# The batch loops of an eight-stage kernel written out, and every wait on a constant

## The reference: what is computed

```python
x = x + tanh(g_xattn[0]) * L0_xattn(ctx, layernorm(x), ...)   # s0: state-space scan over 256 steps
x = x + tanh(g_ffn[0])   * L0_ffn(layernorm(x), ...)          # s1: 8 experts, top 2, and a shared one
x = x + tanh(g_xattn[1]) * L1_xattn(layernorm(x), fside, ctx) # s2: int8-quantised gated product
x = x + tanh(g_ffn[1])   * L1_ffn(layernorm(x), ...)          # s3: ternary SwiGLU
x = x + tanh(g_xattn[2]) * L2_xattn(layernorm(x), ctx, ...)   # s4, sa: 16-head attention
x = x + tanh(g_ffn[2])   * L2_ffn(layernorm(x), ...)          # s5: ternary weights, int8 activations
x = x + tanh(g_xattn[3]) * L3_xattn(layernorm(x), ctx, ...)   # s6: one-head attention
x = x + tanh(g_ffn[3])   * L3_ffn(layernorm(x), ...)          # s7: ternary SwiGLU with a norm
```

## Time and profile before

| | |
|---|---|
| median of 3 runs | 1250.54 us |
| the profiled execution | 1251.78 us |
| its span, first to last instruction | 1249.6 us |
| PE busy | 840.5 us (67%), 4052 matmuls |
| DVE busy | 831.5 us (67%), 1944 instructions |
| ACT busy | 493.4 us (39%), 1242 instructions |
| POOL busy | 371.2 us (30%), 412 instructions |
| mean granted TensorE clock | 0.812 |
| instruction packets | 56 of 8 KB on queue q14, 17 of 16 KB on q8 |

### The profile page before, as it was taken

One profiled execution on the slowest core, in us unless ns is written; L12 is line 12 of the kernel. 1 busy time (PEld: TensorE's weight loads), 2 busy tenths in 40 slices (PEclk: granted clock), 3 DMA queues, 4 the chain that ended last, 5 costly groups with the idle time before them and its releaser, 6 DMA issues.

```text
span 1249.6 us, 15616 instructions
## 1 busy us (share of the span) xinstructions
PE 840.5 (67%) x4052; PEld 618.9 (50%) x4052; DVE 831.5 (67%) x1944; ACT 493.4 (39%) x1242; POOL 371.2 (30%) x412
## 2 busy tenths in 40 slices
PE   2114863587338853785469797879789697888756
PEld 1003641465126621673256585657567485667535
DVE  4896789569875889467630596439863596439763
ACT  2421422224212422243137554545365454555332
POOL 4744362317322553212020122131123212131123
PEclk9555985689558965798589898989999897999857
DMA  3150000010001000023210000010000100000000
GB/s 130 67 233 13 0 1 1 1 47 0 0 0 47 0 0 0 18 84 139 78 53 22 13 1 6 1 35 1 4 1 0 35 0 5 0 21 1 1 0 9
DMA packets 12185, 33.43 MB, mean 27 GB/s; under 512 B 2120, under 2 KB 5584, under 8 KB 10320
## 3 DMA queue, kind: packets, MB, share of 16 engines
q1 hardware_dynamic: 12112, 32.70, 7.5%
HBM read 30.59 MB, written 2.10 MB: 26 GB/s over the span
## 4 chain that ended last, share of the span: by engine, by line
issue 48%; DVE 21%; POOL 14%; PE 10%; ACT 3%; DMA 1%; POOLq 1%; DVEq 1%; SPq 0%; ACTq 0%
PE bk L955 9%; DVE pool L1508 2%; POOL acl L589 2%; DVE pool L1514 2%; POOL pool L557 2%; POOL th L632 2%; POOL ac L595 2%; DVE t L1534 1%; DVE pool L1500 1%; DMA pool<-in_wo 1%; DVE mx L1708 1%; POOL lnr L529 1%; POOL fside L617 1%; POOL first L632 1%; DVE th L1722 1%
## 5 line engine op out<-in xcount | busy, mean ns | idle before, releaser
L557 POOL TENSOR_TENSOR pool<-pool 128x512 f32<-128x512 f32 x64 | 94.0, 1468 | 124.5 <-DVE pool L1514 124.2
L1534 DVE SCALAR_TENSOR_TENSOR t<-th,bk 128x256 f32<-128x256 f32 (+1 forms) x120 | 50.1, 418 | 107.0 <-ACT th L771 105.9
L955 PE MATMUL bk<-hT,first 128*128 128x256 f32 (+1 forms) x448 | 112.8, 399 | 0.0
L762 ACT ACTIVATE ssm_da<-m,nega 128x255 f32<-128x255 f32 x128 | 57.7, 499 | 118.3 <-DVE pool L1508 104.7
L955 PEld LDWEIGHTS bk<-hT,first 128*128 128x128 f32 (+1 forms) x448 | 87.9, 200 | 15.7 <-issue 1.0
L955 PE MATMUL bk<-early,first 128*128 128x256 f32 x384 | 94.8, 384 | 0.0
L955 PE MATMUL bk<-bc,sel 96*128 96x512 bf16 (+1 forms) x128 | 52.7, 418 | 58.2 <-DVE pool L1514 45.4
L1508 DVE TENSOR_TENSOR_SCAN pool<-ssm_da,pool 128x512 f32<-128x512 f32 x64 | 90.3, 1410 | 0.4
L632 POOL TENSOR_TENSOR th<-th,rd 128x256 f32<-128x256 f32 x48 | 29.4, 612 | 189.6 <-DVE rd L1718 189.6
L955 PE MATMUL bk<-first,ac 128*128 128x256 f32 (+1 forms) x224 | 64.8, 414 | 29.7 <-POOL ac L570 29.7
L771 ACT ACTIVATE th<-bk 128x256 f32<-128x256 f32 x88 | 33.9, 385 | 125.6 <-PE bk L955 125.3
(11 more groups left out here) (353 smaller groups left out, 2356.6 us busy)
## 6 DMA issues: line engine op xcount, KB each, us to landing
out<-xo SPq DMA_DIRECT2D x8, 256.0 KB, 2.5
pool<-in_wo SPq DMA_DIRECT2D x4, 512.0 KB, 4.7
first<-in_wq SPq DMA_DIRECT2D x1, 2048.0 KB, 9.1
first<-in_wd SPq DMA_DIRECT2D x1, 1792.0 KB, 16.7
first<-in_wg SPq DMA_DIRECT2D x1, 1760.0 KB, 8.7
first<-in_wu SPq DMA_DIRECT2D x1, 1760.0 KB, 12.5
xin<-in_x SPq DMA_DIRECT2D x4, 256.0 KB, 3.2
pool<-in_q3u SPq DMA_DIRECT2D x1, 1024.0 KB, 5.2
```

The costliest lines, as they stand in the source:

```text
L557: g.tensor_tensor(sy, sy, ssm_u[:, n % 3, :].rearrange("p (e t) -> p e t", e=2), ALU.add).then_inc(*sig("s0.pool", "y", n))
L762: i = s.activation(ssm_da[:, n % 2, e, 1:], sdl[:, e, 1:], ACT.Exp, scale=nega[:, e, n:n + 1])
L955: return t_.matmul(dst, lhsT, rhs, start=start, stop=stop)
L1534: v.scalar_tensor_tensor(out=quarter(t1, c)[0:m, :], in0=quarter(th, c)[0:m, :], scalar=1.0, in1=bank[0:m, 0:S], op0=ALU.add, op1=ALU.mult ...
```

## The change

Each of the five programs loses its two hardware loops: `for b in range(B - 1)` replaces `Fori`, so the first three batches of each phase are written out one behind the other, and `b` is a number everywhere. No instruction of work is added, removed or reordered on any engine; what goes are the loop's counters and branches, and the register instructions ahead of waits and of DMA addresses. SP addresses its DMAs with constant slices.

```diff
@@ SP (line 408), the same in phase_b (line 451)
             def phase_a(b, last):
-                one = slice(B - 1, B) if last else bass.ds(b, 1)
+                one = slice(B - 1, B) if last else slice(b, b + 1)
@@ SP (line 415)
-                    load_ahead(bass.ds(b + 1, 1))
+                    load_ahead(slice(b + 1, b + 2))
@@ SP (line 459)
-                    load_x4(bass.ds(b + 1, 1))
+                    load_x4(slice(b + 1, b + 2))
                     sp.wait_ge(*at(b, "sa.pe", "o", NH - 1))
-                    load_cx(bass.ds(b + 1, 1))
+                    load_cx(slice(b + 1, b + 2))
@@ SP (448, 466), POOL (656, 672), ACT (930, 945), PE (1317, 1333), DVE (1878, 1891)
-            with dve.Fori(0, B - 1) as b:
+            for b in range(B - 1):
                 phase_a(b, True)
             phase_a(B - 1, False)
...
-            with dve.Fori(0, B - 1) as b:
+            for b in range(B - 1):
                 phase_b(b, True)
             phase_b(B - 1, False)
```

More of the change, by code:

```diff
@@ L446, in phase_a @@
                 sp.sem_inc(pace)
-            with sp.Fori(0, B - 1) as b:
+            for b in range(B - 1):
                 phase_a(b, False)
@@ L655, in _ @@
             interleave(s0(0), routes())
-            with pool.Fori(0, B - 1) as b:
+            for b in range(B - 1):
                 phase_a(b, True)
@@ L929, in _ @@
             interleave(s0(0), ternary())
-            with act.Fori(0, B - 1) as b:
+            for b in range(B - 1):
                 phase_a(b, True)
@@ L1316, in _ @@
             interleave(s0(0), ternary())
-            with pe.Fori(0, B - 1) as b:
+            for b in range(B - 1):
                 phase_a(b, True)
```

## The result

The changed kernel took 1236.17 us (median of 4 runs, 1233.93 to 1241.49), the kernel before 1250.41 beside it: a ratio of 0.9887, interval [0.9873, 0.9901]. The forecast was 1243.4, the range 1238 to 1248: right in sign, but the gain is 14.2 us and not 7.1. Where both measurements count, I use their mean, 0.9877.

The account below looks back on a forecast made before the run. The prediction found no single engine filling the span (PE and DVE each busy 67%). Gains of 5.1 + 0.5 + 1.5 = 7.1 us took the median from 1250.54 to 1243.4 us, range 1238 to 1248.

Parts of the forecast that it names:

- Crossings of phase B: DVE's idle at the two taken loop branches between phase B batches, laid to instruction fetch: 5.1 us gained.
- the crossing stays late: Rival: at phase B's crossings something other than DVE is as late as DVE was; 1248.5 us, chance 7%.
- Crossings of phase A: DVE's 3.65 us stall is covered, only PE's own branch counts: 0.26 us, twice, 0.5 us gained.
- SP's load: Issuing the next batch's input sooner in phase A: taken as 0, bounds 0 and 1.9 us.
- PE's pages: 18 more instruction pages to fetch: taken as 0; the rival that they are not hidden, 1289 us, chance 4%.
- Register instructions: Those ahead of waits, in three looped batches of each phase: 1.5 us gained, bounds 0 and 12 us.
- the attention shows it: Argument that most register instructions are hidden: attention took 57.37 us with them in batch 2, 57.42 without in batch 3.
- two chosen steps: Per looped batch: s5's ladder, 0.10 us for each of two halves; s2's wait for POOL's root, 0.15 for each of two products.
- The upper bound of 12 us: Most that all register work could cost: twenty exposed pairs a phase and batch at 0.10 us.
- on the path in many places: Rival: register work is exposed throughout, 12 us instead of 1.5; 1232.9 us, chance 7%.
- The clock: Batches meeting TensorE's clock differently could move each of six crossings by a few tenths either way; only widened the forecast.

Follow-up runs that it names:

- again: The changed kernel itself, unaltered, measured a second time against the kernel before: 1232.96 us, ratio 0.9866.
- reg_three: The changed kernel with the batch number in a register on DVE, POOL and ACT: 1246.45 us, 0.9971 of the kernel before.
- no_end_wait: The changed kernel without POOL's wait at the end of each phase B batch for DVE's last write of x: 1236.51 us, one run.
- reg_written: The changed kernel, all batches written out, with the batch number in a register on every engine: 1248.91 us, 0.9972 of the kernel before.

## Why the prediction was off

- **Crossings of phase B: 5.1 forecast, 4.89 measured.** Right, at the place and by the mechanism named. Nothing else was late behind DVE. The rival "the crossing stays late" is out.
- **Crossings of phase A: 0.5 forecast, 0.55 measured.** `xo` to the first gated product was 7.34 us into batch 1 (251.54 to 258.88 in the trace before) and is 6.93; into batch 2 7.08 and now 6.94. DVE's 3.65 us stall was indeed covered: the wait for ACT grew from 1.90 to 3.50 us in its place (I had said about 5). The matmul follows DVE's result after 0.97 us, where I said 1.2.
- **SP's load and PE's pages: 0 forecast.** Right: registers on SP cost nothing measurable. q8's 15 added pages cost nothing that shows: in `again` the attentions of batches 1 to 3 take 56.96 to 56.98 us, though the code of batches 1 and 2 is fetched anew.
- **Register instructions: 1.5 forecast; about 12 us by the runs with registers written out, and 9.3 by the stages of before and changed (14.7 less the crossings' 4.89 and 0.55). This is the step that failed.** The two figures don't agree, since 12 and the crossings make more than the whole gain: written out, registers cost more than in the loops (the attention of batches 1 and 2 is 57.7 us in `reg_three` and was 57.4 in the loops), and why is open. The step rested on "the attention shows it", 57.37 against 57.42 us. For the attention that was right: with constants and POOL's early start (`no_end_wait`) it takes 57.43 us. The fall to 57.00 us with the change, in the control batch 3 too, is POOL's start. What was wrong is that one stretch was taken to speak for all. Before against changed, s1 gave 4.9 us, 0.55 of them its crossings, and s2 with s3 2.5 where I had 0.9. In written-out code with registers, s5 to s7 are 3.0 to 4.8 us longer and s1 up to 6.1 (`reg_three` against the kernel without registers). And for s1 I compared batch 0 with batch 1, both looped, which could show only what the branch costs, not the registers. The trace before had a row that spoke against it: the router's 0.53 us in all three looped batches and 0.10 in batch 3, whatever part of it is the fetch of code. I held batch 3 against the looped batches at two chosen steps instead of at every step.
- **Of the two steps chosen, one was real.** s5's is 1.24 us now (1044.68 to 1045.92), so 0.10 was right there. s2's was not: the wait for POOL's root is still 0.81 us with constants. Row 611.60 of the earlier trace rows is a 128x1 tile, 461.46 a 128x2. What I took for a register's cost was the shape.
- **The upper bound of 12 us was right**, and the rival built on it (1232.9 us, "on the path in many places") came nearest; I gave it 7%, and the range left it out. It came so near partly by luck: of the 9.3 us, 1.6 are POOL's start in the attention and about 1.8 the clock's edge in batches 0 and 1, against which a dip in batch 2 stands with 2.6. Neither was in its reasoning.
- **The clock, which I let only widen the range,** had a sign. The last group of s1 lay behind the fall to 1.2 GHz in the looped batches before, and being 1.7 us earlier brought it ahead of it, 0.9 us more in batches 0 and 1. In the changed batch 2 a dip took 2.6 us back. Both are within the 14.8 us of the profiles.

Open: how the register instructions' cost divides between their own time, the waits that they lengthen and the places in the code at which pages are fetched; why ACT's register instructions cost 3.0 us beside the others' and about 1.5 alone, with an interval of some 2 us either way; and how much of `reg_written`'s cost in single executions is its last store, which landed after 4.3 us where it took 2.0 in the changed kernel, with one page of q8 beside it (`reg_three` has the same ratio without that).

## What to carry to other kernels

A copy of the loop's body with constants, in the same kernel, is a control for every step of it: pair all steps with the same shape, and sum the differences, before taking a stage that shows none as the answer. Here, register instructions of 40 ns were hidden under long steps and cost up to tenths of a microsecond where short steps on one engine wait for each other, and in s1 these tenths stayed. A stall at one step may belong to its place in the code: move it before blaming the instruction. Where DVE scales a float32 tile while POOL multiplies another, look how close their starts lie; one cheap instruction ahead of POOL's gained as much here as the whole unrolling.

## What the runs showed of the hardware that I had not expected

- A search (FIND_INDEX8) followed by the load of the next values: 0.09 us with a constant wait between, 0.53 with a register instruction of 40 ns there in the loops. With the registers written out instead of looped, it is 0.52, 0.17 and 0.17 in batches 0, 1 and 2: the place in the code counts for 0.36 us of it.
- DVE's scaling of 128x256 float32 takes 0.35 or 0.80 us, by whether POOL's product starts 0.11 us or more, or 0.05 or less, behind it. POOL's own takes 0.61 us beside the slow one and up to 0.72 beside the fast one.
- With the same work ahead of it (PE busy for 7.04 and 7.05 of 9.60 us), TensorE's granted clock dips for 3.4 us in some batches and not in others, and s1 then took 2.6 us more.
- Not all loops paid at the branch: DVE stood 2.6 us at it, PE 0.2. PE's loop code was not fetched again in the later passes (17 pages of q8 looped, 32 written out).
